# Graph kernel on one core: five rotating row buffers in pruning, four in attention, and a store issued with each product

## What is computed

```python
edge_feat = H.T @ V
att = Q @ edge_feat.T * scale * H
att = jax.nn.softmax(att, axis=1)
att_scores = att.mean(axis=0)                       # attention
...
cos = xn @ xn.T
edge_scores = jax.nn.softmax(cos * H / TAU, axis=1)
edge_mask = (edge_scores >= th_edge) & comp_mask[:, None]
H_pruned = H * edge_mask                            # pruning
...
agg = H_pruned.T * dv_isqrt[None, :] @ transformed
agg = agg * de_inv[:, None]
msg = dv_isqrt[:, None] * (H_pruned @ agg)          # gather and scatter
```

## Time and profile before

| | before |
|---|---|
| executions shown | 2624.27, 2627.26, 2629.78 us |
| median | 2627.26 us |
| profiled execution, its own time | 2625.25 us |
| its span | 2623.5 us |
| PE busy | 2146.1 us (82%) |
| DVE busy | 1647.2 us (63%) |
| ACT busy | 768.6 us (29%) |
| DMA moved | 836.03 MB, mean 319 GB/s |
| queue of SP (q1), share of 16 engines | 80.4% |

### The profile page before, as it was taken

How to read it: one execution, slowest core, us unless ns; L and a number is a source line. 1 busy time by engine, 2 the same in 40 slices (tenths; PEclk the granted TensorE clock), 3 DMA queues, 4 the chain that set the end, 5 groups by cost and what they waited for, 6 DMA issues and landing times. The chain is left out here.

```text
span 2623.5 us, 36440 instructions
## 1 busy us (share of the span) xinstructions
PE 2146.1 (82%) x15204; PEld 748.1 (29%) x15224; DVE 1647.2 (63%) x1785; ACT 768.6 (29%) x856; POOL 4.1 (0%) x16
## 2 busy tenths in 40 slices
PE   6769879799776566799999799776666799969998
PEld 2224243232221111244453233221111244432222
DVE  7870043288698888755523288698888755555553
ACT  0010010166443333111110166443333111125554
POOL 0000000000000000000000000000000000000000
PEclk9999989999887887899999999887887899979999
DMA  9958989799389898977779799389898977747770
GB/s 387 424 251 360 408 345 424 321 378 373 145 352 375 357 363 354 375 258 258 274 312 427 323 380 378 152 358 378 356 362 353 369 258 258 285 197 257 262 272 28
DMA packets 119369, 836.03 MB, mean 319 GB/s; under 512 B 8512, under 2 KB 10560, under 8 KB 76608
## 3 DMA queue, kind: packets, MB, share of 16 engines
q1 hardware_dynamic: 117184, 832.63, 80.4%
q10 hardware_dynamic: 2048, 1.35, 0.2%
HBM read 698.68 MB, written 135.27 MB: 318 GB/s over the span
## 5 line engine op out<-in xcount | busy, mean ns | idle before, releaser
L786 DVE CUSTOM_DVE_ANT_0 stream<-ps,stream 128x1024 f32<-128x1024 f32 x504 | 594.3, 1221 | 134.8 <-DMA stream<-in_adj 92.6
L797 ACT ACTIVATE stream<-stream,negmax 128x4096 f32<-128x4096 f32 x128 | 474.9, 3710 | 594.9 <-DVE negmax L791 594.9
L753 PE MATMUL ps<-edgeT,node_twice 64*128 64x512 f32 x1024 | 294.4, 699 | 253.1 <-DVE mx L786 253.1
L401 PE MATMUL ps<-stream,stage 128*64 128x512 f32 x1792 | 401.8, 599 | 62.1 <-DMA stream<-in_adjT 36.5
L1118 DVE SCALAR_TENSOR_TENSOR stream<-stream,cut 128x4096 f32<-128x4096 f32 x62 | 278.0, 4484 | 6.3
L753 PE MATMUL ps<-edgeT,query_twice 64*128 64x512 f32 x1024 | 245.4, 612 | 6.4 <-DVE edgeT L817 3.9
L1078 PE MATMUL ps<-stream,xw 32*64 32x512 f32 x4096 | 229.5, 589 | 0.6 <-ACT xw L1161 0.6
L753 PEld LDWEIGHTS ps<-edgeT,node_twice 64*128 64x128 f32 x1024 | 98.7, 210 | 440.6 <-DVE mx L786 330.4
L401 PEld LDWEIGHTS ps<-stream,stage 128*64 128x64 f32 x1792 | 127.0, 138 | 330.2 <-issue 285.1
L768 PE MATMUL ps<-stream,ones 128*1 128x512 f32 x1024 | 181.0, 844 | 8.2 <-DVE stream L1118 8.2
L1343 ACT ACTIVATE stream<-ps,bits_bias 128x1024 int32<-128x1024 f32 x128 | 142.4, 1114 | 108.1 <-PE ps L1308 107.2
(11 more groups left out here) (180 smaller groups left out, 1461.7 us busy)
## 6 DMA issues: line engine op xcount, KB each, us to landing
stream<-in_adj SPq DMA_DIRECT2D x178, 2048.0 KB, 11.8
stream<-in_adjT SPq DMA_DIRECT2D x74, 2048.0 KB, 12.2
pruned<-stream SPq DMA_DIRECT2D x64, 2048.0 KB, 7.7
spare<-pruned SPq DMA_DIRECT2D x22, 2048.0 KB, 11.2
query_twice<-pruned SPq DMA_DIRECT2D x22, 2048.0 KB, 11.4
node_twice<-pruned SPq DMA_DIRECT2D x20, 2048.0 KB, 11.5
query_twice<-in_adjT SPq DMA_DIRECT2D x7, 2048.0 KB, 35.3
node_twice<-in_adjT SPq DMA_DIRECT2D x7, 2048.0 KB, 35.2
```

The costliest lines, as they stand in the source:

```text
L401: last = nc.tensor.matmul(ps[F * h:F * h + F, bank + b, :], stage[:, t.k % SL, :], half_bank(src, b, h), start=False, stop=False, skip_gro ...
L753: last = nc.tensor.matmul(ps[:, 2 * slot + h, :], stationary[F * h:F * h + F, rows_n], bank_of(edgeT[F * h:F * h + F, :], c), start=True, ...
L786: nc.vector.tensor_tensor_reduce(out=prod[s][:, cols], in0=ps[:, 2 * slot:2 * slot + 2, :].rearrange("p a b -> p (a b)"), in1=block_in[:, ...
L797: nc.scalar.activation(prod[s], prod[s], ACT.Exp, bias=negmax[:, s:s + 1], accum_out=zsum[:, s:s + 1]).then_inc(exp_done, 1)
```

## The change

In pruning `held` has five places instead of three: stream 0 to 2, `spare_block` and `q2`. Four blocks are resident from attention (so `seq` starts at block 22), load 4 is issued at the start, and SP then does for each block: wait for cut n, store n, load n+5. Before, store n was followed by load n+3. Chunk 0 of the gather is issued behind store 28, chunk 1 behind store 29, chunk 2 behind store 31 (before: chunk 0 ahead of store 29, chunk 1 ahead of store 30 and after the last scores, chunk 2 ahead of store 31). The places of the chunks are the same three.

In attention four of these places are used; load n is issued when product n-4 has been made, and load 3 at the start. SP's and VectorE's code is written out in both stages, without the hardware loop; ScalarE keeps it. No computation is changed, and `prod` has three places as before.

```diff
--- before.py
+++ after.py
@@ -735,7 +735,7 @@
         SL3 = 3
         CHUNK = 2 * BANK
         NC = N // CHUNK
-        held = [stream[:, s, :] for s in range(3)]
+        held = [*(stream[:, s, :] for s in range(3)), spare_block, q2[:, :]]
         prod = [stream[:, 3 + s, :] for s in range(3)]
 
         def score_products(pe, t, scores_ready, chunk_used, stationary, operands):
@@ -803,7 +803,8 @@
 
 
             with phase(f"i{it}_attend") as (block, sem):
-                loaded = [sem(f"block_loaded{s}") for s in range(SL3)]
+                HELD = 4
+                loaded = [sem(f"block_loaded{s}") for s in range(HELD)]
                 scores_ready, chunk_used, max_ready = sem("scores_ready"), sem("chunk_used"), sem("max_ready")
                 seen = sem("scores_seen")
                 exp_done, rz_ready, summed = sem("exp_done"), sem("rz_ready"), sem("block_summed")
@@ -823,11 +824,9 @@
 
                 @block.sync
                 def _(sp):
-                    def body(t):
-                        if t.k >= R:
-                            sp.wait_ge(chunk_used, t.n * NC - (SL3 - 1) * NC)
-                            sp.dma_start(held[t.k % SL3], adj_b[t.block]).then_inc(loaded[t.k % SL3], 16)
-                    row_blocks(sp, 3, LEAD, body, seq)
+                    for n in range(R, NB):
+                        wait(sp, chunk_used, (n - (HELD - 1)) * NC)
+                        sp.dma_start(held[n % HELD], adj_b[seq[n]]).then_inc(loaded[n % HELD], 16)
 
                 @block.tensor
                 def _(pe):
@@ -858,11 +857,12 @@
 
                     def body(t):
                         if t.k >= R:
-                            dve.wait_ge(loaded[t.k % SL3], 16 * (t.turn(SL3, R) + 1))
+                            dve.wait_ge(loaded[t.k % HELD], 16 * (t.turn(HELD, R) + 1))
                         wait(dve, summed, t.n - 2)
-                        weighted_scores(dve, t, held[t.k % SL3], seen, scores_ready, chunk_used, max_ready,
+                        weighted_scores(dve, t, held[t.k % HELD], seen, scores_ready, chunk_used, max_ready,
                                         (lambda: reciprocal(t.back(1))) if t.k >= 1 else None)
-                    row_blocks(dve, 3, LEAD, body, seq)
+                    for n in range(NB):
+                        body(last_step(n, seq))
                     reciprocal(last_step(NB - 1, seq))
 
                 @block.scalar
@@ -921,15 +921,16 @@
                         v.tensor_tensor(bank_of(edgeT, k), bank_of(fold4b, k), bank_of(accT, k), ALU.mult)\
                             .then_inc(masked, 1)
 
-                loaded = [sem(f"block_loaded{s}") for s in range(SL3)]
+                HELD = 5
+                loaded = [sem(f"block_loaded{s}") for s in range(HELD)]
                 stored = [sem(f"block_stored{s}") for s in range(SL3)]
                 scores_ready, chunk_used, max_ready = sem("scores_ready"), sem("chunk_used"), sem("max_ready")
                 seen = sem("scores_seen")
                 exp_done, cut_ready, pruned = sem("exp_done"), sem("cut_ready"), sem("pruned")
 
 
-                seq = [23, 24, 25, 26, 27, 28, 29, 30, 31, *range(23)]
-                R, LEAD = 3, 11
+                seq = [*range(22, NB), *range(22)]
+                R, LEAD = 4, 11
 
                 summed, rows_ready, deg_ready, inverse_ready, copies_ready, copies_taken = (
                     sem(n) for n in ("block_summed", "edge_sums_taken", "edge_sums_ready", "edge_inverse_ready",
@@ -956,32 +957,10 @@
                     return (n + 8) % NB
 
                 def buffer(t):
-                    if t.k < R:
-                        return held[(t.k + 2) % SL3]
-                    return spare_block if t.k == R else held[(t.k + 1) % SL3]
+                    return held[t.k % HELD]
 
                 @block.sync
                 def _(sp):
-                    def store(t):
-                        s = t.k % SL3
-                        sp.wait_ge(pruned, t.n + 1)
-                        sp.dma_start(Hp[t.block], prod[s]).then_inc(stored[s], 16)
-
-                    def load(t):
-                        sp.dma_start(buffer(t), adj_b[t.block]).then_inc(loaded[t.k % SL3], 16)
-
-                    def body(t):
-
-
-                        if t.k >= SL3:
-                            store(t.back(SL3))
-                        if t.k in (3, 4, 5):
-                            load(Step(t.n + 1, t.k + 1, None, 3, seq))
-                        if t.k >= 7:
-                            load(t)
-                    load(Step(3, 3, None, 3, seq))
-                    row_blocks(sp, 3, LEAD + 3, body, seq)
-
                     def load_chunk(x):
                         g, c = divmod(x, CH)
                         rows_c = slice(first_row(c), first_row(c) + 8)
@@ -989,21 +968,29 @@
                                      Hp[rows_c].rearrange("n p j -> p n j")[:, :, BANK * g:BANK * g + BANK])\
                             .then_inc(chunk_loaded[x % 3], 16)
 
-                    for s in range(SL3):
-                        sp.wait_ge(stored[s], 16 * 3)
-                    load_chunk(0)
-                    store(last_step(NB - 3, seq))
-                    for s, n in enumerate((6, 6, 5)):
-                        sp.wait_ge(stored[s], 16 * n)
+                    def wait_stored(blocks):
+                        for s in range(SL3):
+                            sp.wait_ge(stored[s], 16 * len(range(s, blocks, SL3)))
+
+                    def load(n):
+                        sp.dma_start(held[n % HELD], adj_b[seq[n]]).then_inc(loaded[n % HELD], 16)
+
+                    load(R)
+                    for n in range(NB):
+                        sp.wait_ge(pruned, n + 1)
+                        sp.dma_start(Hp[seq[n]], prod[n % SL3]).then_inc(stored[n % SL3], 16)
+                        if n + HELD < NB:
+                            load(n + HELD)
+                        if n == 28:
+                            wait_stored(10)
+                            load_chunk(0)
+                        if n == 29:
+                            wait_stored(18)
+                            load_chunk(1)
+                    wait_stored(26)
                     sp.wait_ge(scores_ready, NB * NC)
-                    load_chunk(1)
-                    store(last_step(NB - 2, seq))
-                    for s, n in enumerate((9, 8, 8)):
-                        sp.wait_ge(stored[s], 16 * n)
                     load_chunk(2)
-                    store(last_step(NB - 1, seq))
-                    for s in range(SL3):
-                        sp.wait_ge(stored[s], 16 * len(range(s, NB, SL3)))
+                    wait_stored(NB)
                     for x in range(3, groups * CH):
                         sp.wait_ge(gathered, x - 2)
                         sp.wait_ge(turned, x - 2)
@@ -1123,7 +1110,7 @@
                     def body(t):
                         s = t.k % SL3
                         if t.k >= R:
-                            dve.wait_ge(loaded[s], 16 * (t.turn(SL3, R) + 1))
+                            dve.wait_ge(loaded[t.k % HELD], 16 * (t.turn(HELD, R) + 1))
                         wait(dve, stored[s], t.turn(SL3) * 16)
                         wait(dve, summed, t.n - 2)
                         weighted_scores(dve, t, buffer(t), seen, scores_ready, chunk_used, max_ready)
```

## The result

The changed kernel takes 2559.24 us (median of 4 executions, 2556.59 to 2569.88), the kernel before 2627.56 in the same comparison: a ratio of 0.9749, 95% interval 0.9719 to 0.9778, or 68 us less. Forecast were 2560.0. The profiled execution took 2560.11 us, where the sum had 2558.3 (its span, 2558.3 us, is a different quantity: it went from 2623.5 to 2558.3, 65 us less).

The account below looks back on a forecast made before the run. Late adj loads held VectorE in pruning; with the change the DMA engines would bind. Pruning's 68.7 us less attention's 1.7 gave 67.0 off 2625.25, 2558.3; with the median 2.0 above that execution, 2560; range 2526 to 2598.

Parts of the forecast that it names:

- Loads are no longer waited for, stores are: Pruning: product waits on adj loads fall from 92.6 us to near 0; store waits of about 1 us a block replace them.
- The DMA engines become the bound: Pruning: one store and one load take 10.3 us a block, more than VectorE's 9.37 us.
- 51 transfers at 407 GB/s: First pruning stage: stores 1 to 26 and loads 6 to 30, 5.15 us each, take 262.7 us.
- a deep queue carries more: Rival, pruning: 4.80 us a transfer with no gap between store and load, gain 52.2 us a stage, time 2525; chance 0.14.
- slower: Rival, pruning: product n+3 waits for store n; landings over 13.8 us lose time, at 15 us 2661 in all; chance 0.06.
- The argument that a load issued behind a store doesn't slow it: Pruning, said against the slower rival: a store lands in 7.4 us now with a load right behind it.
- Hidden under the queue's 10.3: Pruning: written-out code takes VectorE's pair from 9.63 to 9.37 us, counting only with a faster queue.
- Attention +0.8 us a stage: Attention: 24 more blocks written out cost 0.035 us each, 1.7 us for both stages.
- Attention's fourth place 0: Attention: no product waits for a load there, so the fourth place by itself brings 0.
- the chunks 0 with 5 us of cover: Gather's start: chunk 2 behind the last store lands some 14 us after the cut, read at 19.6 us; cost 0.
- No gain: Rival, pruning: stores and loads together can't keep over 360 GB/s for long; time 2629; chance 0.07.
- TensorE as the bound: Rival, pruning: TensorE at 1.2 GHz takes 10.9 us a block, time 2603; chance 0.10, shared with a rate in between.

Follow-up runs that it names:

- experiment 3: The changed kernel with four places for blocks and four for products in pruning, gather chunks moved, ScalarE's pruning code written out: 2539.39 us.
- experiment 5: The changed kernel with load n+5 issued ahead of store n instead of behind it: 2680.46 us.
- experiment 6: The changed kernel with the stores of pruning issued by ScalarE into its own queue, ScalarE's pruning code written out: 2643.68 us.
- experiment 1: The kernel before with SP's and VectorE's code written out in attention and pruning, buffers and queue order as before: 2620.81 us.
- experiment 10: The changed kernel with VectorE's attention code in a hardware loop of 12 blocks again: 2557.25 us.
- experiment 2: The changed kernel with four places for blocks of adj in pruning instead of five, chunks 0 and 1 exchanging places: 2561.3 us.

## Why the prediction was right, and where it wasn't

**The number** came out within 1 us, and part of that is luck: the rate of 407 GB/s was put down to the engines, which carried 429 with one product place more, and another chain happens to take as long.

- *Loads are no longer waited for, stores are*: right. 92.6 us to none, and 36.9 us in 51 waits, 0.7 us each, forecast "about 1 us a block".
- *"The DMA engines become the bound", 51 transfers at 407 GB/s*: right in size (10.15 us for 10.3, last cut 1034.1 for 1034.0, 34.4 and 34.1 us a stage for 34.35) and wrong as the cause. The rate of 413 was a result, not a limit: with one more product place the same engines carried 429 (experiment 3), and with the same bytes in another order the block took 12.4 us (experiment 5). The bound is the store's way to its landing over a rotation of three products. Why the stretches that I took the rate from showed nearly this rate isn't shown; they were the same mix at about this depth of the queue.
- *Rival "a deep queue carries more"*: said to be against the share of 1.0. It exists (9.69 / 2 = 4.85 us a transfer in experiment 3, forecast 4.80, for which no row stood); what kept it from the changed kernel is the number of product places, not of row places.
- *Rival "slower"*: not this kernel, but its formula is the law above. Its point of 13.8 us, from which on the stage is slower than before, nearly held: a mean of 13.7 us (experiment 6) gave 0.6% more than before, 14.8 us (experiment 5) 2%. The argument that a load issued behind a store doesn't slow it is right for one queue and false for two.
- *"Hidden under the queue's 10.3", the loop's 0.26 us in pruning*: wrong. Written out alone it brought 4.1 us a stage (experiment 1). So of the 68 us about 5 come from the code's form and the rest from the queue, if the two add up; the new order with the loop kept wasn't run.
- *Attention +0.8 us a stage*: +0.8 and +1.9, and the cause is the written-out code (experiment 10).
- *Attention's fourth place 0; the chunks 0 with 5 us of cover*: right, the last transpose starts 243.7 us behind the cut before and 243.4 after, the next attention 429.8 us in both. Chunk 2 was issued at 1034.64, 0.5 us after the cut, and the third transpose wasn't held up:

```profile
1034.64 0.85 SPq L967 DMA_DIRECT2D node_twice<-pruned  x1
...
1049.60 4.40 DVE L1174 STREAM_TRANSPOSE stream<-query_twice 128x4096 f32<-128x4096 f32 x1
1053.92 4.40 DVE L1174 STREAM_TRANSPOSE stream<-node_twice 128x4096 f32<-128x4096 f32 x1
```

- *Five places for blocks*: four would have done (experiment 2). I never asked what each of the two added places is worth.
- *No gain, TensorE as the bound*: neither. The Trainium skill ("DMA: Bandwidth & Descriptors", "Where 436 GB/s comes from") has some 358 GB/s for HBM to SBUF as what binds; this core kept 429 GB/s of loads and stores over 165 us, near the 435 that the section gives for the ports. The kernel runs on one core alone; what two at a time would get, no run shows.

## What to carry to other kernels

When buffers rotate and a transfer sits between two uses of one, write the chain down: the time of a block is (landing + issue + compute between) / (blocks that the chain spans, here the places less one), for the load's ring and for the store's ring apart, and the slower ring decides. A landing holds everything that stands ahead in the queue, so put first what is waited for soonest: here two exchanged lines were worth some 120 us. And share places between the rings: five for blocks and three for products left 20 us that four and four took.

## What the runs showed that I had not expected

The DMA share isn't a measure of room. The packets of row blocks have 16384 bytes; from the trace's own records, 800 to 960 us:

```
kernel             median ns  mean ns  over 700 ns  GB/s
before                611       653      10.1%        361
changed               611       636       6.9%        413
5 load first          611       723      20.8%        338
3 four products       611       613       0.5%        430
```

16 engines with one packet of 611 ns each are 429 GB/s. A slow packet counts as busy all its time, so the share reads 1.00 at 413 GB/s as well as at 430. In experiment 3, where a store has one and a half transfers ahead of it at its issue, nearly all packets take 611 ns. What makes the others slow stays open. It isn't the start after an empty queue: in the kernel before, 334 of the 357 slow packets begin 4 to 7 us behind the issue of a store, 284 of the 357 while 16 packets are under way, and of the 967 packets in the first 3 us behind a store's issue, where the queue often starts again after a pause, 3 are slow. Five places for blocks together with four for products was not tried either: there is no ninth place.
